# Building count tables for a graph sum: two of a unit's four 128-column comparisons on GpSimd, and a chunk's row numbers loaded 28 at a time

## The reference, cut to what matters

```python
deg  = segment_sum(ones_like(dst), dst, n);  dinv = where(deg > 0, rsqrt(deg), 0)
norm = dinv[src] * dinv[dst]
out  = segment_sum(xw[src] * norm[:, None], dst, n) + b      # once after W1, once after W2
```

## Time and profile before

| | us |
|---|---|
| median of 3 runs | 4388.67 |
| lowest, highest | 4383.09, 4389.2 |
| span of the profiled execution | 5825.1 |
| in it, stage `build_counts_and_sum`, first L743 to last L810 | 138.9 to 773.8 |
| in it, `load_counts_and_sum` | from about 800 to 1122 |

### The profile page before, as it was taken

One profiled execution on the slowest core, in us unless ns is written; L12 is line 12 of the kernel. 1 busy time (PEld: TensorE's weight loads), 2 busy tenths in 40 slices (PEclk: granted clock), 3 DMA queues, 4 the chain that ended last, 5 costly groups with the idle time before them and its releaser, 6 DMA issues. The chain is left out here.

```text
span 5825.1 us, 61632 instructions
## 1 busy us (share of the span) xinstructions
PE 3173.4 (54%) x16208; PEld 1958.6 (34%) x16208; DVE 3165.7 (54%) x10115; ACT 2409.4 (41%) x5229; POOL 2312.0 (40%) x2409
## 2 busy tenths in 40 slices
PE   2888787623555555562155554555523555564563
PEld 1333343312333333342033333333311333343342
DVE  5999853513454554576064464555822455454466
ACT  0766630023444444443143443444433444444453
POOL 3000002074555455415545545544064545545422
PEclk7999998856777677786577777777756777777786
DMA  2111124221212222111112212211021212212110
GB/s 75 60 60 60 60 85 168 99 62 36 48 46 48 47 47 50 42 28 37 42 45 48 52 44 48 50 46 44 4 55 37 47 47 47 50 45 47 45 25 23
DMA packets 127624, 298.46 MB, mean 51 GB/s; under 512 B 45412, under 2 KB 74972, under 8 KB 123712
## 3 DMA queue, kind: packets, MB, share of 16 engines
q0 software_dynamic: 74976, 155.58, 11.6%
q1 hardware_dynamic: 52320, 139.24, 7.1%
HBM read 241.28 MB, written 53.38 MB: 51 GB/s over the span
## 5 line engine op out<-in xcount | busy, mean ns | idle before, releaser
L1400 POOL DMA_INDIRECT work<-table,lane_src x2184 | 2072.7, 949 | 1897.4 <-PE psum L1554 967.3
L1439 ACT ACTIVATE work<-work,middle_node_number 128x384 f16<-128x384 f16 x1587 | 958.0, 604 | 1997.8 <-DMA work<-table,lane_src 950.8
L1497 PE MATMUL psum<-work 128*128 128x396 bf16 (+1 forms) x5850 | 1360.1, 380 | 699.7 <-issue 464.9
L1554 PE MATMUL psum<-work 128*128 128x136 f32 x4836 | 827.7, 339 | 1004.9 <-DVE node_sums L1722 890.6
L1722 DVE TENSOR_TENSOR node_sums<-node_sums,psum 128x136 f32 x2418 | 561.3, 294 | 1455.8 <-remote 892.2
L1554 PEld LDWEIGHTS psum<-work 128*128 128x128 f32 x4836 | 778.8, 242 | 1085.0 <-issue 969.9
L1497 PEld LDWEIGHTS psum<-work 128*128 128x128 bf16 x5850 | 626.3, 109 | 1290.0 <-issue 758.1
L1442 ACT ACTIVATE work<-work 128x384 bf16<-128x384 f16 x1587 | 829.4, 523 | 50.4
L715 PE MATMUL psum<-work 128*128 128x448 f16 x2100 | 460.9, 358 | 47.4 <-issue 37.5
L744 DVE TENSOR_SCALAR work<-work 128x400 f16<-128x400 f16 x1568 | 468.3, 320 | 0.0
L772 PE MATMUL psum<-work 128*128 128x400 f16 x1568 | 342.1, 342 | 111.8 <-DVE work L744 90.9
(11 more groups left out here) (360 smaller groups left out, 2539.9 us busy)
## 6 DMA issues: line engine op xcount, KB each, us to landing
counts<-work SPq DMA_DIRECT2D x14, 2800.0 KB, 8.1
work<-counts SPq DMA_DIRECT2D x14, 2800.0 KB
work<-table,lane_src POOLq DMA_INDIRECT x2184
work<-spread SPq DMA_DIRECT2D x78, 256.0 KB
work<-masks SPq DMA_DIRECT2D x78, 128.0 KB
work<-source_rows SPq DMA_DIRECT2D x39, 192.0 KB
spread<-node_sums SPq DMA_DIRECT2D x4, 896.0 KB
table<-work SPq DMA_DIRECT2D x10, 330.0 KB
```

Of the source, the lines that this page charges most:

```text
L1400: pool.indirect_dma_start(m.ring[:, s % SLOTS, 0:F + H], None, m.d_table[H], bass.IndirectOffsetOnAxis(ap=m.src[:, s:s + 1], axis=0)).then ...
L1439: act.activation(away, rows_of(g, u), ACT.Abs, bias=m.low_tile[:, hi:hi + 1]).then_inc(far_known, 1)
L1497: mm = pe.matmul(aid_banks[:, k, 0:3 * (F + H)], hot_of(g, u)[:, k * P:(k + 1) * P], m.all_thirds[:, :, hi, 0:F + H], start=(hi == 0), sto ...
L1554: pe.matmul(sum_slot(s), m.onehot[b % 2][:, s % U, :], m.ring[:, s % SLOTS, :], start=True, stop=True).then_inc(product, 1)
```

## The change

Two things are changed, in `allocate` and in `build_counts_and_sum`.

- GpSimd makes the low one-hots of blocks 0 and 1 of each unit (PAIRED = 2), with the same comparison into the same buffer. VectorE makes that of block 2 alone. GpSimd's program is written out, 392 times a wait for `unit_done` and two comparisons, and counts up a new semaphore `lo_paired`, for which TensorE waits as well.
- CREGS is 28: the registers are loaded once a chunk, at k = 0. `cj_row` is allocated ahead of `count_row`, so at word 30848, a multiple of 16 bytes.

```diff
-CREGS = 14
+CREGS = 28
...
+PAIRED = 2
...
     late = 4 * 8 * LANES + 8 * P + 9 * P
+    m.cj_row = m.arena[0:1, late:late + CG * P].bitcast(I32)
+    late += CG * P
     m.count_row = m.arena[:, late:late + EDGE_TILES]
     late += EDGE_TILES
-    m.cj_row = m.arena[0:1, late:late + CG * P].bitcast(I32)
-    late += CG * P
...
                     for b in range(CB):
-                        if b < CB - 1:
+                        if PAIRED <= b < CB - 1:
                             dve.tensor_scalar(m.hot_lo[:, d, b, :], m.iota_cols[:, 0:P], m.low[:, b, bass.ds(n, 1)], None, ALU.is_equal)
...
+        @block.gpsimd
+        def _(pool):
+            for n in range(CUNITS):
+                if n >= DEPTH:
+                    pool.wait_ge(unit_done, n - (DEPTH - 1))
+                for b in range(PAIRED):
+                    t = pool.tensor_scalar(m.hot_lo[:, n % DEPTH, b, :], m.iota_cols[:, 0:P], m.low[:, b, n:n + 1], None, ALU.is_equal)
+                t.then_inc(lo_paired, 1)
...
                     pe.wait_ge(hot, n + 1)
+                    pe.wait_ge(lo_paired, n + 1)
                     pe.wait_ge(lo_hot, n + 1)
```

More of the change, by code:

```diff
@@ L721, in build_counts_and_sum @@
 def build_counts_and_sum(nc, m):
-    ph, (hot, lo_away, lo_hot, unit_done, evacuated, stored0, stored1, produced, summed) = phase(
-        nc, "onehots_done", "last_low_distance", "last_low_onehot", "unit_counted", "unit_evacuated", "chunk_stored_0", "chunk_stored_1", "chunk_product", "unit_summed")
+    ph, (hot, lo_paired, lo_away, lo_hot, unit_done, evacuated, stored0, stored1, produced, summed) = phase(
+        nc, "onehots_done", "first_lows_onehot", "last_low_distance", "last_low_onehot", "unit_counted", "unit_evacuated", "chunk_stored_0", "chunk_stored_1", "chunk_product", "unit_summed")
     stored = (stored0, stored1)
```

## The result

The changed kernel takes 4279.27 us (median of 4 runs, 4275.01 to 4281.18) against 4386.89 (4 runs, 4383.09 to 4389.2): ratio 0.9754, 95% interval 0.9741 to 0.9768. That is 107.6 us faster. The prediction had 45 us: the direction was right, the time lies in the range, and the gain was more than twice the forecast.

A forecast was written before the change was run, and what follows sets the result against it. VectorE was taken to bound the counts stage at 1.50 us a unit. Shorter units (-17 us) and register loads (-28 us) made -45 us, from 4388.7 to 4343 us; range 4270 to 4450.

The forecast's parts named there:

- What bounds the stage: Counts stage: everybody waits for VectorE, whose unit takes 1.50 us; 392 units take 588 of 635 us.
- The next limit: Counts stage, behind VectorE: TensorE at 1.26 us in 25 of 28 units, 1.20 on average; ScalarE at most 1.15.
- The cost of GpSimd's comparisons: Counts stage: each GpSimd comparison takes 0.37 us and pushes VectorE back by 0.145, making its unit 1.46 us.
- the upper end: GpSimd's comparison of 128 columns alone: 0.257 us plus 108 more columns at the two-input rate, 0.48 us.
- the 17: Counts stage: gain from shorter VectorE units, 392 x (1.46 - 1.50) = -17 us.
- The break-even: Counts stage: each comparison moved rids VectorE of 0.163 us and gives it 0.145, so the change nearly breaks even.
- The loads in the counts stage: 28 registers load in 2.1 us: -9 us at eight ordinary stalls, -14 us at four loop heads.
- The next stage: Stage after the counts: sums and loads covered by TensorE's 75 matmuls, 14 us; nothing counted before its end.
- The tails: Last sums of the counts stage and of the next: shorter loads save 2.4 us each, -5 us together.
- GpSimd didn't set the unit: Rival, counts stage: GpSimd keeps VectorE out over 0.28 us, or sets the unit; 4439 or 4457 us; chance 0.26.
- the second: Rival, counts stage: VectorE and GpSimd disturb each other only in two-input sums, not comparisons; -143 us, 4246; chance 0.11.
- the third: Rival, register loads: the long load stays at single reads, 6.4 us; +43 us, 4432; chance 0.07.

The follow-up runs named there:

- e_nobody: Changed kernel, but nobody makes the low one-hots of blocks 0 and 1, so GpSimd idles in the counts stage: 4221.17 us, ratio 0.9623.
- e_add: Loads-alone kernel plus two GpSimd comparisons of 128 columns a unit into a buffer nobody reads: 4410.91 us, executed once.
- e_add32: Loads-alone kernel plus two GpSimd comparisons of 32 columns a unit into a buffer nobody reads: 4349.89 us, executed once.
- e_one: Changed kernel, but GpSimd makes one of four low one-hots instead of two: 4282.94 us, ratio 0.9766.
- e_place: Changed kernel, but the row numbers stay at their old place, 8 bytes past a multiple of 16: 4421.23 us, executed once.
- e_pool: Kernel before with only the comparisons changed, two of four on GpSimd, loads still 14 at a time at the old place: 4326.86 us, ratio 0.9868.
- before_again: The kernel before, unchanged, profiled once more: 4386.27 us, span 4384.5 us.
- e_touch: Loads-alone kernel plus two GpSimd comparisons in all at the stage's start; 5852.88 us, ratio 0.9936, on a chip where before takes 5889.56.

## Why the prediction was right or wrong

**In short.** The change was taken for -45 us and gave -107.6. The step that missed most is the price of GpSimd's comparison to VectorE, put at 0.145 us and measured at 0.107 (24 of the 63 us). Behind it stand the next stage, put at nothing but for its last sums and measured at -19.1 us (17), the stalls at the loads of the counts stage (14), and the time behind the stages (9).

**What bounds the stage: right.** VectorE's unit of 1.50 us, its parts of 0.163, 0.235 and 0.08, and the 1.175 us left without two comparisons were measured to the hundredth in `e_nobody`. The next limit was right as well: I had TensorE at 1.26 us in 25 of 28 units, and it takes 1.24 to 1.25 there.

**The cost of GpSimd's comparisons: the mechanism was half right, its size wrong, and two errors partly cancelled.** I took 0.37 us for the instruction from half the two-input rate, with 0.48 as the upper end; it takes 0.595, outside both ends, at 2.5 ns a column (`e_add`, `e_add32`). And I took it that from GpSimd's turn to its end VectorE is shut out. With the true 0.595 that would have been 0.595 - 0.13 - 0.085 = 0.38 us for each, a unit of 1.94 and a kernel some 140 us slower than before; it was 0.107. That the direction came out right is luck to that extent. In the trace after, a whole L744 stands inside a GpSimd record of the least length. What VectorE loses goes with the columns, 0.8 ns for each. So the unit came to 1.39 instead of 1.46: 41 us instead of 17 over the 392 units (56 of them 1.421 to 1.337, 336 of them 1.500 to 1.392; the 17 is 16 by its own factors). This also speaks against the Trainium skill's lock for the whole instruction ("SBUF — State Buffer", "Who interferes with whom"), in comparisons at least: the sharing is there, as it says, and the price of the whole instruction is not. By that rule the changed kernel would have been slower than before.

**The break-even: wrong as a consequence.** I wrote that each comparison moved trades 0.163 for 0.145 us. It trades 0.163 for 0.107, and one alone for 0.016 beside the sums (`e_one`).

**The loads in the counts stage: right in kind, too small in size.** Reads of four on a multiple of 16 bytes held (1.85 us against 2.1; `e_place` from the old place 6.25). I had -23 us for the stage; all that is not unit time is 77.7 - 41 = 37 us. The loads alone gave 15.7 of it, since at the loop's head the load stays behind the store and takes 6 us, not 4.4. I had charged the store's delay to each read, so that seven reads would pay half of what 14 do; measured, the store adds 4.1 us to the load in seven reads and 4.5 to the one in 14. GpSimd's part alone (`e_pool`) gave 52.3 - 41 = 11 us beyond its units. The last 10 come only when both are made: with VectorE's unit shorter, the store comes no longer ahead of the load, and the load at the loop's head falls from 6 to 2.8 to 3.9 us. I had reckoned the two parts apart.

**The next stage: the step that failed outright.** Apart from its last sums I counted nothing, "covered by TensorE's 75 matmuls". It gave 19.1 us, 16.7 of them by the loads alone. The cover holds for chunks in which VectorE has sums only. In two of the 14 chunks it doesn't: VectorE has other work in front (the search for the steps' tiles ahead of the fifth product, the edge masks ahead of the twelfth), its sums come late, and TensorE waits 4.9 and 6.7 us for them. Waits of `before_again` from 855 to 1080 us:

```profile
PE psum L715 <- DVE node_sums L709: 11.6, 2, 6.7
PEld psum L715 <- issue: 18.8, 19, 7.2
```

In the kernel after, from 774 to 981 us, the first is gone and the second is 5.1 us.

**The tails: right.** -3.1 us at the end of the counts stage and -2.3 at the end of the next, where the last product is followed by 8.4 us instead of 10.7; I had -2.4 for each. The second is counted with its stage.

**Behind the stages: -8.9 us, not foreseen**, 7 of them in the gathers of one layer.

**The rivals.** None took place. GpSimd didn't set the unit, though its instruction was longer than my upper end; the second, without any sharing, would have given the 165 us of `e_nobody`; the third fell with the load at 1.85 us. The sum of the misses: 41 - 17 = 24 us in the units, 37 - 23 = 14 in the stage's stalls, 17 in the next stage, 9 behind, 64 us, against 107.6 - 45 = 63.

## What to carry to other kernels

When an engine's cover is used to cost an edit at nothing, look at the cover chunk by chunk: it fails where the engine has other work in front. Work moved to GpSimd from a VectorE that is the bound can pay although each holds the other up; what counts is what VectorE loses for it (here 0.11 us for an instruction of 0.6), and adding the instruction to an otherwise unchanged kernel, into a buffer that nobody reads, measures that by itself. When two engines have nearly the same unit, read both timelines: an engine that runs ahead into its buffers looks faster than the stage is. Lay out lists that are loaded into registers on multiples of 16 bytes, and load them when no large store is in flight.

## What the runs showed of the hardware

- A register load of 28 words took 1.85 us on a multiple of 16 bytes and 6.25 us 8 bytes past one. Where a store of 2800 KB moved its data within the load, it took 11.0 us 8 bytes past; issued one to two microseconds behind the store, 28 words on a multiple took 6.0 us and 14 words 8 bytes past one 7.7.
- A GpSimd comparison of f16 with one number for each partition took 0.593 us at 128 columns and 0.355 at 32, and cost VectorE's comparisons beside it 0.09 to 0.11 us at 128 columns and at most 0.02 at 32.
- The first layer of gathers was 8 ns a gather slower (0.952 against 0.944 us) in every kernel in which GpSimd had made no comparison before it. What changes is not known.
- Chips differ: the kernel before took 4385 us on some and 5889.56 on one. There the 728 gathers of the first layer stretched over 1334 us in `e_touch` instead of 913, though a gather's own record was as short (0.947 us); GpSimd waited in between. The first profile of the kernel before, with 1315 us for that layer, looks like that chip; which it ran on isn't recorded.
